# A two-layer decoder on one core: products of constants, a split load issue, and statistics gathered in the loops of the second and fifth stages

## The reference, cut to what matters

```python
x = x + _L0_attn_ref(_layernorm(x), ...)        # self-attention, 16 heads of 128
x = x + _L0_xattn_ref(_layernorm(x), ctx, ctx)  # cross-attention, 32 heads of 8
x = x + _L0_ffn_ref(_layernorm(x), ...)         # attention as a modulation, then a gated feed-forward
x = x + _L1_attn_ref(_layernorm(x), ...)        # running sums over the sequence
x = x + _L1_xattn_ref(_layernorm(x), ctx, ctx, ...)  # cross-attention, 16 heads of 16
x = x + _L1_ffn_ref(_layernorm(x), ...)         # gated feed-forward with 4-bit weights
```

```python
scores = einsum('bkgsd,bktd->bkgst', qh, kh) / sqrt(8)
out = einsum('bkgst,bktd->bkgsd', softmax(scores, -1), vh)
```

## Time and profile before

| | us |
|---|---|
| runs shown, median (lowest to highest) | 1947.82 (1945.99 to 1949.38) |
| profiled execution, its own time | 1944.22 |
| its span, first to last instruction | 1942.4 |
| PE busy in the span | 1711.3 |
| DVE busy | 1134.2 |
| ACT busy | 842.3 |
| POOL busy | 686.1 |
| mean granted clock of PE | 0.902 |

### The profile page before, as it was taken

One profiled execution on the slowest core, in us unless ns is written; L12 is line 12 of the kernel. 1 busy time (PEld: TensorE's weight loads), 2 busy tenths in 40 slices (PEclk: granted clock), 3 DMA queues, 4 the chain that ended last, 5 costly groups with the idle time before them and its releaser, 6 DMA issues. The chain is left out here.

```text
span 1942.4 us, 33715 instructions
## 1 busy us (share of the span) xinstructions
PE 1711.3 (88%) x12986; PEld 1324.9 (68%) x12986; DVE 1134.2 (58%) x1820; ACT 842.3 (43%) x1399; POOL 686.1 (35%) x508
## 2 busy tenths in 40 slices
PE   4999999999959996889999786899998297999997
PEld 3888888888846665668788562444444275788886
DVE  6676767676765555565322495999897666211111
ACT  3555555555533433444422325555562275322222
POOL 0111221122123431640122204999996341223232
PEclk9999999999975555789999896999999598899999
DMA  3011111111120002000000000000000440000001
GB/s 94 15 58 55 63 38 57 54 62 38 57 98 2 1 2 92 2 2 2 2 1 1 19 18 0 1 1 1 0 1 0 157 146 2 1 1 1 1 0 43
DMA packets 49490, 57.56 MB, mean 30 GB/s; under 512 B 7216, under 2 KB 43568, under 8 KB 49248
## 3 DMA queue, kind: packets, MB, share of 16 engines
q1 hardware_dynamic: 49376, 55.97, 8.9%
HBM read 41.28 MB, written 14.68 MB: 29 GB/s over the span
## 5 line engine op out<-in xcount | busy, mean ns | idle before, releaser
L543 POOL TENSOR_TENSOR s_w_parts<-s_w_raw,s_w_parts 128x768 fp32r<-128x768 f32 x16 | 29.7, 1854 | 428.8 <-ACT s_w_parts L495 428.8
L1293 DVE TENSOR_TENSOR s6f_hid<-s6f_act_sb,s6f_u_ps 128x512 f32<-128x512 f32 x64 | 44.0, 687 | 219.5 <-PE s6f_u_ps L1244 219.5
L1316 POOL TENSOR_TENSOR s6f_hid_parts<-s6f_hid,s6f_hid_parts 128x512 fp32r<-128x512 f32 x64 | 82.7, 1293 | 230.5 <-ACT s6f_hid_parts L1282 230.5
L1826 POOL TENSOR_TENSOR s4b_pcs<-s4b_cs,s_p_rows 128x1024 f32<-128x1024 f32 x64 | 120.8, 1913 | 95.4 <-ACT s4b_cs L1872 95.4
L1837 POOL TENSOR_TENSOR s4b_with_re<-s4b_with_re,s4b_with_im 128x1024 f32<-128x1024 f32 x64 | 150.9, 2385 | 2.6 <-DVE s4b_with_im L1791 2.6
L1912 PE MATMUL s4b_c_ps<-s4b_pcs,const 128*128 128x512 f32 x256 | 122.3, 600 | 0.0
L419 PE MATMUL s_v_ps<-s_wv_parts,s_xnT 128*128 128x256 f32 x768 | 103.8, 285 | 12.0 <-ACT s_v L524 6.4
L478 PE MATMUL s_o_ps<-s_w_parts,s_zT 128*128 128x256 f32 x768 | 110.2, 294 | 4.1 <-DVE x_rows L582 4.1
L419 PEld LDWEIGHTS s_v_ps<-s_wv_parts,s_xnT 128*128 128x128 f32 x768 | 96.3, 191 | 17.6 <-ACT s_v L524 9.7
L1902 PE MATMUL s4b_turns_ps<-s_theta_bd,s_zc 128*128 128x512 f32 x128 | 78.1, 694 | 31.4 <-DVE s4b_frac L1776 30.4
L1316 POOL TENSOR_TENSOR s3f_hid_parts<-s3f_hid,s3f_hid_parts 128x512 fp32r<-128x512 f32 x32 | 41.3, 1291 | 180.2 <-ACT s3f_hid_parts L1282 180.2
(11 more groups left out here) (305 smaller groups left out, 4138.4 us busy)
## 6 DMA issues: line engine op xcount, KB each, us to landing
stored_weights<-s1q_halves SPq DMA_DIRECT2D x16, 768.0 KB, 3.5
s6w_parts<-stored_weights SPq DMA_DIRECT2D x32, 384.0 KB, 7.5
s1q_packed<-in_codes SPq DMA_DIRECT2D x8, 384.0 KB, 4.3
s1q_scale<-in_scale_rows SPq DMA_DIRECT2D x8, 384.0 KB, 5.0
x_rows<-in_x SPq DMA_DIRECT2D x1, 2048.0 KB, 8.2
s_w_raw<-in_L_attn_W_Q SPq DMA_DIRECT2D x16, 128.0 KB, 2.2
s_w_raw<-in_L_attn_W_K SPq DMA_DIRECT2D x16, 128.0 KB, 2.4
s_w_raw<-in_L_attn_W_O SPq DMA_DIRECT2D x16, 128.0 KB, 2.4
```

Source lines behind the costliest of these rows:

```text
L1293: nc.vector.tensor_tensor(hid[:, f % 2, :], act_sb[:, f % 2, :], u_ps[:, f % 2, :], ALU.mult) \
L1316: nc.gpsimd.tensor_tensor(hid_parts[:, f % 2, 1, :], hid[:, f % 2, :], hid_parts[:, f % 2, 0, :], ALU.subtract).then_inc(low_done, 1)
L1826: last = nc.gpsimd.tensor_tensor(pcs[:, half, n_, :].rearrange("p (k c) -> p k c", k=HK), cs[:, half, n_, :].rearrange("p (k c) -> p k c", ...
```

## The change

Four edits. (1) The second stage issues only the first chunk of the context before its barrier; SP issues the other three in the main block. (2) PE of the second stage multiplies constants, `ident` by `age`, into `o_ps`, whose content is overwritten later: four products at step 2, one behind the scores of unit 0 and one behind those of unit 1. (3) DVE's loop of the second stage makes the `bn_stats` of a tile of the result at lag 7, behind the two additions to it, and the stage sets `core.stats_ready`. (4) The fifth stage does so too, at lag 6, one step behind `finish`.

```diff
-        def load_context(sp):
-            for n in range(NT // CHUNK):
+        def load_context(sp, first=0, last=1):
+            for n in range(first, last):
...
+            @block.sync
+            def _(sp):
+                load_context(sp, 1, NT // CHUNK)
...
-                run_steps(dve, U, [(shift, 3), (attended, 5)], unroll=2, head=U + 5)
+                def gather_stats(u, rnd, n):
+                    if u % 2:
+                        dve.wait_ge(added, u + 1)
+                        nc.vector.bn_stats(core.stats[:, u // 2, :], core.x[:, u // 2, :])
+
+                run_steps(dve, U, [(shift, 3), (attended, 5), (gather_stats, 7)], unroll=2, head=U + 7)
+                core.stats_ready = True
...
+                def keep_busy(first, later):
+                    def part(u, rnd, n):
+                        if not isinstance(u, int) or u > 1:
+                            return
+                        for _ in range(later if u else first):
+                            nc.tensor.matmul(o_ps[:, :], core.c("ident"), core.c("age"), start=True, stop=True)
+                    return part
...
-                run_steps(pe, U, [(scores, 3), (weigh(0), 5), (turn(0), 4), (weigh(1), 5), (turn(1), 4),
+                run_steps(pe, U, [(keep_busy(4, 0), 2), (scores, 3), (keep_busy(1, 1), 3), (weigh(0), 5), (turn(0), 4), (weigh(1), 5), (turn(1), 4),
...
-            steps(dve, [(attended, 4), (shift, 2)] + ([(spread_values, 1)] if own else []) + [(finish, 5)])
+            def gather_stats(i, rnd, k):
+                dve.wait_ge(f_out, i + 1)
+                nc.vector.bn_stats(core.stats[:, i, :], core.x[:, i, :])
+
+            steps(dve, [(attended, 4), (shift, 2)] + ([(spread_values, 1)] if own else []) + [(finish, 5)] +
+                  ([] if own else [(gather_stats, 6)]))
...
                     prefetch=prefetch)
+        core.stats_ready = True
```

## The result

The changed kernel takes 1880.18 us, the median of four runs (1877.49 to 1881.84); the kernel before took 1948.6 beside it (1945.99 to 1949.42). The ratio is 0.965, with a 95% interval of 0.9633 to 0.9666. The forecast was 1878 us, the range 1866 to 1903. The profiled execution took 1879.44 us, its span 1877.7.

What follows compares the result with a forecast made beforehand. PE at 1.2 GHz in the second stage was taken as the bound. Gains 65.5 + 0 - 0.5 + 4.6 = 69.6 us took the profiled 1944.22 to 1874.6; against the median 1947.82 the forecast was 1878 us, range 1866 to 1903.

Steps and rivals of the forecast that it cites:

- The likeliest case of the forecast: Whole kernel: the second stage's clock rises and holds; 1868 to 1893 us, chance 77%.
- the split: Second stage's start: six load issues moved behind the barrier open the main block 3.3 us earlier, at cost 0.
- the fifth stage's gather: Fifth stage's loop: statistics hidden in DVE's wait save 5.32 us at the sixth's start, less 0.7; gain 4.6 us.
- four products outlast the time that the rise takes: Second stage's start: four products, 7 us cold, outlast the 4.9 to 5.9 us until the higher clock level.
- Rival B: Second stage: the clock holds only for a part, a long pause losing it; falling halfway gives 1911 us; chance 8%.
- where PE waits: Second stage, first units: the two later products stand in PE's idle time, 2.73 us between scores 0 and scores 1.
- The kernel before never gets it: Second stage: a stage that lost the clock would not regain it, as the kernel before never does in 180 us.
- the stage would fall back to the low level: Second stage: by the skill's rule on transposes the clock falls back; part of the 12% rival of no lasting rise.
- both chains as named: Second stage's pair: DVE's subtraction to scores, 3.40 us; every second unit ACT's copy of xT, 3.65; together 7.05 us.
- the lower bound of 6.80: Second stage: a pair of units takes 6.80 us if the copy of xT is hidden; 3.6 us better over the stage.
- either row: Earlier trace's two clock rises, in other stages: higher level about 5.9 us and 4.9 us after the work begins.
- The gather in the second stage: Second stage's loop: statistics cost 0, gain 0 at the third stage because SP ends last; 0.5 us lost at the end.

Runs made afterwards that it cites:

- experiment 2: Kernel before plus the six products of constants, nothing else: 1887.58 us, all four runs high.
- experiment 5: Changed kernel without the two later products, the four ahead of the first transposes kept: 1938.38 to 1945.15 us, five of five runs low.
- experiment 12: Changed kernel with only the two later products, the third stage's small load issues moved behind its barrier, and turn_x placed earlier in PE's step: 1872.06 us.
- experiment 9: Changed kernel with the third stage's small load issues moved behind its barrier: 1876.3 us, eight runs.
- experiment 8: Changed kernel with all eight loads of the context issued ahead of the second stage's barrier, as in the kernel before: 1882.11 us.
- experiment 3: Changed kernel without the statistics in the second stage's loop; they are made at the third stage's start again: 1879.01 us.
- experiment 10: Changed kernel with the third stage's small load issues moved behind its barrier and without the statistics in the second stage's loop: 1879.94 us, nine runs.
- experiment 4: Changed kernel without the statistics in the fifth stage's loop: 1883.44 us, four runs.
- experiment 7: Changed kernel with only the two later products, without the four ahead of the first transposes: 1879.5 us, five of five runs high.
- experiment 6: Changed kernel with two products ahead of the first transposes in place of four, the two later ones kept: 1880.4 us, five of five runs high.

## Why the prediction was right, and where its reasons were not

**The time.** 1880.2 against 1878. Of the 68.4 us (1948.6 less 1880.2) some 61 are the level (1948.97 less 1887.65, the kernel before at either) and 7.5 the rest (1887.65 less 1880.18). The likeliest case of the forecast came true. The 7.5 are not fully accounted for: taken out singly the split, the fifth stage's gather and the second's are worth 1.9, 3.3 and -1.2 us, 4.0 together, while experiment 2, which lacks all three, is 7.4 above the changed kernel. The groups differ by enough to leave this open.

**Why the clock rises: the wrong step.** The prediction had four products outlast the time that the rise takes, and the stage's own work then hold it, with "the second stage shows no such pause now". The first half is as the traces show: the level comes 4 us behind the first product (forecast 4.9 to 5.9). The second half is wrong. The pause is in the earlier trace rows, 2.73 us between scores 0 and scores 1, and I had read it as room for a product and not as a danger to the clock; in experiment 5's trace the clock falls at its end, and five of five runs are low. Rival B's mechanism was right, its place was the first units, and its price was all of the gain. The two later products were costed at nothing, "where PE waits"; the cost is right, and the gain of some 60 us hangs on them. The time came out right because the change had them in it, for a reason that the prediction did not give: that part is luck. With the four products alone its reasoning would have forecast the same gain, and experiment 5 has none of it.

**"The kernel before never gets it."** It does, in 10 of 40 runs. Three runs and one trace of before could not show that; but they could not show "never" either. The change is worth 68 us against the common run of the kernel before and 7.5 against its lucky one. The rule of the Trainium skill (TensorE: Matmul & The Clock Gate, Part 4) is that a transpose-mode product does not count as busy for the clock in the same way. By it, the prediction said, the stage would fall back to the low level. That did not happen where the pause was filled: from 576 to 690 us the clock reads 1.00 in each of eleven windows, and transposes (1.31 us of turn and half of 0.38 of turn_x) are some 1.5 of the 3.5 us of PE's work in a unit. Experiment 5 is what the rule would forecast, but with the same mix of transposes behind the pause; what differs is the pause.

**The pair.** 7.14 us for a forecast of 7.05, by both chains as named; the 0.69 us for the scores, taken from the earlier trace rows, was the right duration. Experiment 12 bears out the lower bound of 6.80 (copy of xT hidden) with 6.83. The stage is 118.9 us for 117.3, 1.6 more: 14.5 pairs at 0.09 more make 1.3 of it.

**The start.** First scores at 576.76 for 577.7: the clock rises a microsecond sooner than either row had it, and the products take 5.60 us for 6.0 to 6.5. How soon it rises varies: in the eight traces with four products in front it comes 2.9 us (experiment 9) to 6.2 us (experiment 2) behind the first of them, estimates from the 2 us windows. The 4.9 us read from the earlier trace rows is also counted from the end of a wait of 1.69 us; PE's work there begins at 1539.50, 12 us ahead of the rise. The load split is real but its size is 2 to 4 us (experiment 8).

**The gather in the second stage.** Gain 0 at the third stage with SP last: right, by the wait of 8.31 us and by experiment 3, and with its reason shown by experiments 9 and 10. In the loop it is hidden, as forecast: the pair is 7.14 us with it and without.

**The gather in the fifth stage.** 3.3 us for 4.6, in two ways: experiment 4, and the traces' lead growing from 60.4 to 63.8 us across the fifth stage. The term was too large by 1.3 us. Why stays open: in the changed kernel's tail PE runs below its full clock for a few microseconds (0.91 in 1560 to 1580), where the kernel before has 1.00 until 1638, but experiment 4's trace, without this gather, reads 0.89 in the same window.

**The sum.** The profiled execution is 64.8 us under its counterpart (1944.22 to 1879.44) where 69.6 were forecast. By the leads, the changed kernel is 0.7 short at the third stage's first rows (64.3 for 65.0: 1.6 in the length of the second stage, less the 0.9 of the sooner first scores), gains 0.5 in the third, loses 4.4 in the fourth, which the change does not touch, is 1.2 short in the fifth and gains 0.9 in the sixth: 4.9 in all. The median of the runs, 68.4 better, has no such loss.

## What to carry to other kernels

Where a stage sits at the low clock although the same work runs at the high one elsewhere, look at its first few microseconds, not at its mean: a wait of 2.73 us right behind the rise lost the clock for the whole stage here, and work without use brought the whole gain inside that wait and nothing that shows ahead of it. Take several runs of the kernel before as well, since a kernel near such an edge has two times, and a change of tens of microseconds may only fix which of them one gets. Work moved off an engine ahead of a barrier gains nothing until the last arriver, here a row of DMA issues, is moved too; do both or measure neither.

## What the runs showed of the hardware that I had not expected

- The clock has two lasting levels at this mix. With PE busy 19.05 of 20 us it stays at 0.50 for the whole stage (experiment 5), and with the same work, busy 17.73 of 20 us, it stays at 1.00 (the changed kernel). Both are steady for over 100 us, and which of them it is was settled 6 to 13 us behind PE's first work: the clock fell at 582.0 in experiment 5 and rose at 577.7, 584.0 and 584.8 in experiments 7, 12 and 6, where PE had begun at 571.6 to 572.8.
- The choice can be chance: one program without products came out at 1875.13 and at 1946.51 us, and one later product gave seven high and three low runs of ten.
- Three small transfers issued right behind eight large ones hold SP for 5.5 to 6.4 us together (5.45 in experiment 12, 5.69 in 3, 5.94 in 9, 6.01 in the kernel before, 6.38 in the changed one), where each of the eight large ones took 0.38 to 0.89. Where DVE had taken longer, so that they were issued 5 us after the eighth (experiment 10, at 707.47), the same three took 1.31 us. Why is not shown.
